# A transformer block in one kernel: one low half made by VectorE in two pairs, the z split moved into the fourth pick, and the last two tiles' roots by Sqrt and one Newton step

## The reference

```python
x  = hidden_states                              # 2048 tokens x 512, f32
d  = x @ gate_w.T - local_point                 # width 128
a  = x @ up_w.T @ local_approx.T + sum_m ((sign d)^m |d|^m / m! * (x @ up_w.T) [* (|d| <= 2.5) if m > 4]) @ fuse_m.T   # m = 1..6
f  = silu(x @ ffn_gate_w.T) * (x @ ffn_up_w.T) @ ffn_down_w.T          # width 1248
x1 = layernorm(x + a + f)
s  = x1 @ c1.T @ c2.T                           # rank 16, 1792 columns
idx = argmax of s in each block of 32 columns   # 56 winners per token
h  = relu(w1[idx] . x1)
out = layernorm(x1 + h @ w2t[idx])
```

## Time and profile before

| | us |
|---|---|
| time before, median of 3 runs (719.85 to 720.08) | 719.88 |
| the profiled execution's own time | 720.04 |
| its span, first to last instruction | 718.2 |
| TensorE busy | 705.4 (98%) |
| VectorE busy | 527.7 (73%) |
| ScalarE busy | 267.5 (37%) |
| GpSimd busy | 293.1 (41%) |

### The profile page before, as it was taken

How to read it: one execution, slowest core, us unless ns; L and a number is a source line. 1 busy time by engine, 2 the same in 40 slices (tenths; PEclk the granted TensorE clock), 3 DMA queues, 4 the chain that set the end, 5 groups by cost and what they waited for, 6 DMA issues and landing times.

```text
span 718.2 us, 10310 instructions
## 1 busy us (share of the span) xinstructions
PE 705.4 (98%) x3949; PEld 380.4 (53%) x3949; DVE 527.7 (73%) x983; ACT 267.5 (37%) x451; POOL 293.1 (41%) x278
## 2 busy tenths in 40 slices
PE   8999999999999999999999999999999999999996
PEld 3444444444444444444444456666666666667763
DVE  6979897796887779677778878948885778337236
ACT  1575457435721221222112224434334333443341
POOL 0452443211111161334215576897366435742330
PEclk9999999999999999999999999999999999999999
DMA  9637319300000110110010222121222101220101
GB/s 325 260 139 198 59 13 377 80 21 39 1 15 19 22 21 0 35 20 20 6 16 19 50 49 50 40 54 16 50 74 64 47 4 59 61 45 2 58 2 59
DMA packets 40833, 44.67 MB, mean 62 GB/s; under 512 B 25296, under 2 KB 33104, under 8 KB 39888
## 3 DMA queue, kind: packets, MB, share of 16 engines
q1 hardware_dynamic: 37808, 39.29, 18.0%
q0 software_dynamic: 2112, 4.19, 3.5%
q10 hardware_dynamic: 864, 0.53, 0.2%
HBM read 34.33 MB, written 4.42 MB: 54 GB/s over the span
## 4 chain that ended last, share of the span: by engine, by line
PE 73%; DVE 7%; POOL 5%; issue 2%; ACT 1%; DMA 0%; POOLq 0%; DVEq 0%; ACTq 0%
PE acc L544 27%; PE pb L524 14%; PE pa L524 13%; PE pb L778 7%; PE pa L778 6%; PE acc L621 2%; PE acc L867 1%; DVE big L1707 1%; POOL work L1127 1%; PE pick_a L687 1%; PE pick_b L687 1%; POOL quad L1181 1%; DVE small L1596 1%; POOL big L1134 1%; DVE big L1705 1%
## 5 line engine op out<-in xcount | busy, mean ns | idle before, releaser
L544 PE MATMUL acc<-big,work 128*128 128x512 f16 x1038 | 235.2, 379 | 1.5 <-POOL work L1127 1.5
L1127 POOL TENSOR_TENSOR work<-work 128x512 f16<-128x512 f32 x92 | 110.4, 1212 | 274.1 <-ACT work L1013 214.3
L544 PEld LDWEIGHTS acc<-big,work 128*128 128x128 f16 x1038 | 101.4, 98 | 117.3 <-POOL work L1127 2.0
L524 PE MATMUL pa<-xs,big 128*128 128x512 f16 x480 | 111.2, 379 | 0.0
L524 PE MATMUL pb<-xs,big 128*128 128x512 f16 x480 | 110.1, 379 | 0.0
L1838 DVE TENSOR_TENSOR pa<-pa,big 128x512 f32<-128x512 f32 x28 | 19.6, 699 | 83.4 <-ACT big L1093 69.0
L524 PEld LDWEIGHTS pa<-xs,big 128*128 128x128 f16 x480 | 46.1, 98 | 54.1
L524 PEld LDWEIGHTS pb<-xs,big 128*128 128x128 f16 x480 | 46.0, 98 | 53.4
L621 PE MATMUL acc<-big 128*128 128x512 f16 x336 | 73.8, 379 | 0.4 <-DVE big L1443 0.2
L1013 ACT ACTIVATE work<-work 128x512 f16<-128x512 f32 x40 | 25.2, 629 | 111.5 <-DVE work L1580 111.5
L1134 POOL TENSOR_TENSOR big<-work,big 128x512 f16<-128x512 f32 x27 | 36.8, 1378 | 64.1 <-ACT big L949 63.8
(11 more groups left out here) (214 smaller groups left out, 981.5 us busy)
## 6 DMA issues: line engine op xcount, KB each, us to landing
big<-in_w_all SPq DMA_DIRECT2D x2, 3840.0 KB, 17.4
big<-in_x_t SPq DMA_DIRECT2D x16, 256.0 KB, 8.2
rows<-in_x POOLq DMA_DIRECT2D x4, 1024.0 KB, 11.9
big<-spread_rows SPq DMA_DIRECT2D x16, 256.0 KB, 5.9
big<-in_w_all SPq DMA_DIRECT2D x2, 1536.0 KB, 11.5
big<-spread_rows SPq DMA_DIRECT2D x16, 192.0 KB, 5.1
out<-rows SPq DMA_DIRECT2D x3, 1024.0 KB, 4.4
big<-in_w_all SPq DMA_DIRECT2D x1, 2048.0 KB, 14.7
```

The lines of the kernel that those rows point to most:

```text
L524: mm = nc.tensor.matmul(dst[:, :], weights(wp)(kc * P, P), x_part16(g, xp, kc), start=(kc == 0 and wp == xp), stop=(kc == KC - 1 and wp == 1))
L544: mm = nc.tensor.matmul(acc[t][:, :], act_part(pair, j, ap, t * P, P), weights(wp)(0, H), start=(first and ap == wp), stop=(last and ap == 1))
L1127: nc.gpsimd.tensor_tensor(act_part(pair, j, 1), act32[j], act_part(pair, j, 0), ALU.subtract).then_inc(act_lo, 1)
```

## The change

1. **A low half by VectorE.** `LOW_BY_DVE = (4, 5)`. For sparse units 4 and 5 VectorE makes the low half of j = 0 (`low_first`) and raises a new semaphore `first_lo`, for which TensorE waits ahead of that product. In unit 4 it stands behind the low half of x1, in unit 5 between two picks. GpSimd makes j = 1 alone, after a wait for `first_lo`, and raises `act_lo` by two.
2. **The z split moves.** `pick` is cut in two, `find_hits` and `rank_hits`. In units 9, 12, 14, 17 and 18 the z split of the next tile stands between them in pick 3; that next unit has none at its head.
3. **The last two tiles.** The inverse square root of tile 2 and of tile 3 comes from ScalarE's Sqrt of variance + eps, VectorE's reciprocal and one Newton step (three instructions). ScalarE runs one Sqrt on a constant ahead of its last rows, and its order becomes: rows of tiles 0 and 1, root of tile 2, rows of tile 2, root of tile 3. VectorE takes and measures half 0 of the last tile inside the work on tile 2. Tiles 0 and 1 keep `size_rows`.

```diff
+LOW_BY_DVE = (4, 5)
...
-                    pe.wait_ge(act_lo, N1 + before * 2 + j + 1)
+                    if j == 0 and before in LOW_BY_DVE:
+                        pe.wait_ge(first_lo, LOW_BY_DVE.index(before) + 1)
+                    else:
+                        pe.wait_ge(act_lo, N1 + before * 2 + j + 1)
...
+            def root(t):
+
+                act.wait_ge(ve_ready, t - 1)
+                act.activation(ya[:, t:t + 1], ve[:, t:t + 1], ACT.Sqrt).then_inc(root_ready, 1)
+
+            act.activation(c1_inv, const_sb[:, 4:5], ACT.Sqrt, scale=0.0)
+            act.wait_ge(rows_sized, 1)
+            scale_row(0)
+            scale_row(1)
+            root(2)
+            act.wait_ge(rows_sized, 2)
+            scale_row(2)
+            root(3)
...
-                    else:
+                    elif n not in LOW_BY_DVE:
                         low(GROUPS * U1 + n, j, m)
+                    elif j:
+                        pool.wait_ge(first_lo, LOW_BY_DVE.index(n) + 1)
+                        low(GROUPS * U1 + n, j, m, 2)
...
-                cut_z(tile, pick_a)
+                if g * U1 + u - 1 not in JOB_IN_SWIGLU or u == 2:
+                    cut_z(tile, pick_a)
                 swiglu(g, u, 0)
...
                 if nxt is not None:
-                    pick(tile, 3, pick_b)
+                    find_hits(tile, 3, pick_b)
+                    if g * U1 + u in JOB_IN_SWIGLU and g * U1 + u < GROUPS * U1 - 1:
+                        cut_z(nxt, pick_a)
+                    rank_hits(tile, 3)
...
+            def low_first(n):
+
+                pair = GROUPS * U1 + n
+                dve.wait_ge(act_hi, N1 + 2 * n + 1)
+                v.tensor_tensor(act_part(pair, 0, 1), act32[0], act_part(pair, 0, 0), ALU.subtract).then_inc(first_lo, 1)
...
+                if n in LOW_BY_DVE and n not in PICKS_AT:
+                    low_first(n)
                 if n in PICKS_AT:
                     tile, k = PICKS_AT[n]
                     pick(tile, k, pick_a)
+                    if n in LOW_BY_DVE:
+                        low_first(n)
                     pick(tile, k + 1, pick_b)
...
+            size_rows(0, 2, rows_sized)
+            take(3, sparse_ready, hid_out, [2])
+            moments(3, 2, [2])
+            start_root(2)
+            take_half(0)
+            invert_root(2)
+            size_half(0)
+            refine_root(2)
+            v.scalar_tensor_tensor(out=row_shift[:, 2:3], in0=mv[:, 2, 0:1], scalar=-1.0, in1=y[:, 2:3],
+                                   op0=ALU.mult, op1=ALU.mult).then_inc(rows_sized, 1)
+            take_half(1)
+            size_half(1)
             settle()
-            step(v.bn_aggr(mv[:, TPG - 1, :], small[:, (TPG - 2) * 6:TPG * 6]))
-            size_rows(TPG - 1, TPG)
+            step(v.bn_aggr(mv[:, TPG - 1, :], small[:, 0:2 * 6]))
+            start_root(3)
+            invert_root(3)
+            refine_root(3)
```

More of the change, by code:

```diff
@@ L326, in program @@
         act_lo, peak_ready, term_lo = sem("act_lo"), sem("peak_ready"), sem("term_lo")
+        first_lo = sem("first_lo")
         fuse_lo = sem("fuse_lo")
@@ L339, in program @@
         rows_sized, last_row_out = sem("rows_sized"), sem("last_row_out")
+        ve_ready, root_ready = sem("ve_ready"), sem("root_ready")
         W1_BEFORE = 2
@@ L1114, in _, with scale_row, low @@
                     hidden(g, u)
-            for t in range(TPG - 1):
+            def scale_row(t):
                 tile = (GROUPS - 1) * TPG + t
-                act.wait_ge(rows_sized, max(t, 1))
                 act.activation(rows[:, tile, :], rows[:, tile, :], ACT.Identity, bias=row_shift[:, t:t + 1],
                                scale=y[:, t:t + 1]).then_inc(rows_out, 1)
+            def root(t):
[9 more added lines that the diff above has]
+            root(3)
         @block.gpsimd
         def _(pool):
-            def low(pair, j, n):
+            def low(pair, j, n, halves=1):
                 pool.wait_ge(act_hi, n + 1)
-                nc.gpsimd.tensor_tensor(act_part(pair, j, 1), act32[j], act_part(pair, j, 0), ALU.subtract).then_inc(act_lo, 1)
+                nc.gpsimd.tensor_tensor(act_part(pair, j, 1), act32[j], act_part(pair, j, 0), ALU.subtract).then_inc(act_lo, halves)
             def terms_low(g):
@@ L1693, in cut_z, with find_hits @@
                 v.tensor_tensor(pieces(6, 2), wide(z_rest, 2), pieces(3, 2), ALU.subtract).then_inc(z_cut, 1)
-            def pick(tile, k, src):
+            def find_hits(tile, k, src):
                 q = tile * PICKS + k
@@ L1700, in pick @@
                 h = hit[b].rearrange("p (b j) -> p b j", j=SPARSITY)
-                r = rank[b].rearrange("p (b j) -> p b j", j=SPARSITY)
                 dve.wait_ge(score_ready, q + 1)
@@ L1705, in pick, with rank_hits @@
                 v.tensor_tensor(h, s, block_max[b].unsqueeze(2).broadcast_to([P, PB, SPARSITY]), ALU.is_equal).then_inc(score_used, 1)
+            def rank_hits(tile, k):
+                q = tile * PICKS + k
+                b = k % 2
+                h = hit[b].rearrange("p (b j) -> p b j", j=SPARSITY)
+                r = rank[b].rearrange("p (b j) -> p b j", j=SPARSITY)
                 dve.wait_ge(score_used, PICKS + q + 1)
@@ L1713, in pick @@
                     step(last)
+            def pick(tile, k, src):
+                find_hits(tile, k, src)
+                rank_hits(tile, k)
             def w2_low(c0, c1):
@@ L1875, in _, with start_root, invert_root @@
                     normalise(g - 1, rows_out, mask=(g, u + 1))
-            for t in range(TPG - 1):
+            def start_root(t):
+                settle()
+                v.tensor_scalar(ve[:, t:t + 1], mv[:, t, 1:2], EPS, None, ALU.add).then_inc(ve_ready, 1)
+                step(v.tensor_scalar(spare[:, t:t + 1], mv[:, t, 1:2], EPS, -0.5, ALU.add, ALU.mult))
+            def invert_root(t):
+                dve.wait_ge(root_ready, t - 1)
+                step(v.reciprocal(y[:, t:t + 1], ya[:, t:t + 1]))
@@ new lines, in refine_root, with take_half @@
+            def refine_root(t):
+                y_, ya_ = y[:, t:t + 1], ya[:, t:t + 1]
+                settle()
+                step(v.tensor_tensor(ya_, y_, y_, ALU.mult))
+                settle()
+                step(v.tensor_tensor(ya_, ya_, spare[:, t:t + 1], ALU.mult))
+                settle()
+                step(v.scalar_tensor_tensor(out=y_, in0=ya_, scalar=1.5, in1=y_, op0=ALU.add, op1=ALU.mult))
+                settle()
+            def take_half(h):
+                r = rows[:, GROUPS * TPG - 1, h * HALF:(h + 1) * HALF]
+                dve.wait_ge(sparse_ready, GROUPS * TPG + h)
+                v.scalar_tensor_tensor(out=r, in0=last_halves[h], scalar=hid_out, in1=r,
+                                       op0=ALU.mult, op1=ALU.add).then_inc(banks_added, 1)
@@ L1877, in _, with size_half @@
+            def size_half(h):
+                dve.wait_ge(banks_added, added(2, GROUPS - 1, TPG - 1) + h)
+                step(v.bn_stats(stats[:, h, :], rows[:, GROUPS * TPG - 1, h * HALF:(h + 1) * HALF]))
+            for t in range(2):
                 take(3, sparse_ready, hid_out, [t])
                 moments(3, 2, [t])
[L1879 to L1887, removed]
+            size_rows(0, 2, rows_sized)
```

## The result

The changed kernel takes 715.56 us (median of 5 runs, 715.17 to 715.94) against 719.88 before (5 runs, 719.85 to 720.39). The ratio is 0.9933 with a 95% interval of 0.9921 to 0.9944, which puts the time at 715.1. The forecast was 716.2 with a range from 715.5: the direction and all three places were right, and the change won more than was forecast, so that by the ratio the time lies under the range (the median by itself, 715.56, lies just inside it). In the profiled execution (715.60 us, span 713.8) 4.44 us are gone from the span, where I had summed 3.85.

The account below looks back on a forecast made before the run. Bound: TensorE's own stream, with waits for one transposition and two low halves, plus the end behind its last product. 720.04 - 1.4 (z split) - 1.45 (low halves) - 1.0 (end) = 716.2 us; range 715.5 to 717.9.

Parts of the forecast that it names:

- TensorE, free since 398.79 (400.24 - 1.45): Before unit 18's scores: TensorE was taken as idle 1.45 us, waiting for the z transposition, until 400.24.
- Gain 0.76 + 0.69 = 1.45: Sparse units 4 and 5: TensorE's waits for GpSimd's low halves of pairs 4 and 5 both go, winning 1.45 us.
- the 0.05 that I had left standing at the z split: Unit 17: remainder of TensorE's 1.45 us wait for the transposition after the forecast gain of 1.4.
- all of it, 1.45: Upper bound for the gain in unit 17: TensorE's whole wait of 1.45 us goes.
- The z split: Unit 17: split starts 1.49 us earlier, at 394.41, GpSimd holds it about 0.1, done 1.39 earlier; gain 1.4.
- the wait goes all the same: Unit 17's transposition took 3.2 us, median 2.2; if what held it strikes elsewhere, TensorE's wait still goes.
- I cost these moves at nothing.: Splits moved in the other four units cost 0: rank and winner, 1.49 us, fit VectorE's 1.51 idle.
- the first rival: Unit 18: gating product uses up its 1.23 us reserve, giving back 0.1 to 1.0; 716.3 to 717.2; no separate chance.
- The low halves: Sparse units 4 and 5: VectorE's subtraction holds GpSimd up to 0.69 us per unit, within TensorE's reserve; gain 1.45.
- The end: Last tiles: half 1 starts 0.5 us earlier, ten root steps shrink from 1.79 to 1.28; gain 1.0, bounds 0.5 and 1.15.
- price without the cover of half 0 would be 0.5: Last tiles: without half 0 running beside tile 2's Sqrt, the new end would cost 0.5 us.
- the slower rival: Five moved splits make VectorE wait inside pick 3, TensorE then waits for gating products: 6.9 us lost, 723.1; chance 0.04.

Follow-up runs that it names:

- e6_roots: Kernel before with only the roots of tiles 2 and 3 by Sqrt and one Newton step, last tile's halves in the old order: 718.71 us, ratio 0.9976.

## Why the forecast came out low

- **What bounds the kernel.** Right: TensorE's stream, three waits in it, and the stretch behind it. 3.39 of the 4.44 came from the waits and 1.15 from the stretch; 0.10 was given back by the start-up.
- **"TensorE, free since 398.79 (400.24 - 1.45)" and "Gain 0.76 + 0.69 = 1.45".** This is the step that failed, in size only. I took the idle column for the length of a wait. Start to start the waits were 1.61, 0.93 and 0.86. With the 0.05 that I had left standing at the z split this is 0.54 of the sum's shortfall of 0.59 (the end adds 0.15, the start-up takes 0.10), and it also capped my bounds ("all of it, 1.45"), so that the range stopped too early. By the ratio 4.8 us were won (4.0 to 5.7); the rest of the distance to the 4.44 of the traces lies inside that interval and is not explained.
- **The z split.** The mechanism was right: start at 394.4, held once by GpSimd for 0.21 (I took 0.1), done 1.31 earlier by the trace and 1.41 against TensorE, whose products stand 0.10 later here. Against a wait of 1.61 that would have left 0.2; the landing took 2.7 us and not 3.2 and closed it. I had written that the wait goes all the same if the delay strikes elsewhere. It struck the same tile and cost less, which I had not foreseen, so here the forecast mechanism had help. (Tiles 10 and 11 in the last parts of the prediction should read 9 and 10: unit 18 routes tile 9.)
- **"I cost these moves at nothing."** Right for units 9, 12 and 14 and wrong for 18. Alone, the move in 17 loses 0.86 again one unit later. That is the first rival at work, by a cause that I had not named in it: not the gating product, but the next z split at its old place. The change was spared it because it moved that split too.
- **The low halves.** Both waits went and none came back. The lock was there, as the Trainium skill has it ("SBUF — State Buffer", "Who interferes with whom"): 1.21 for VectorE's subtraction against the 0.69 of the earlier trace rows, and 1.06 for a GpSimd pass. It lay in TensorE's reserve. Its price for GpSimd was 0.33 in unit 4 and 0.44 in unit 5, against my 0.69. (GpSimd's j = 1 was due at 481.4 by my own terms, not at 481.3; nothing hung on it.)
- **The end.** 1.15 against 1.0, within the bounds. Half 1 starts on time (0.58 won, 0.5 forecast), the root costs 1.20 and not 1.28 (0.59 won, 0.5 forecast); the reciprocal took 0.16 (I took 0.2) and the hand-overs 0.03 and 0.04. The text's "price without the cover of half 0 would be 0.5" is wrong: e6_roots has no such cover and loses nothing.
- **The rivals.** No rival came true in the whole change. The end did not hand its gain to ScalarE: the small step, Sqrt and both hand-overs take 0.42 (709.60 to 710.02). (The border of the slower rival should read 5.1, 721.3 - 716.2, and not 5.3.)

## What to carry to other kernels

Size a wait of a pipelined engine by the distance from start to start, set against the same pair of instructions at a place with no wait; the idle column takes its beginning from a modelled end, and here hid 0.16 or 0.17 us of each of the three waits. When one late step is moved forward, look at the next instance of the same step: the engine that was freed arrives there earlier too, and meets it at its old place. And before two edits to one chain are credited with a sum, try each: here the shorter roots alone gave all of it, and the reordering alone cost 0.33.

## What the runs showed of the hardware

A round trip from VectorE to ScalarE and back with a one-column Sqrt costs 0.42 us with the first VectorE instruction in it, little more than two small VectorE steps at 0.195. The table load of 1.28 us is followed by the first Sqrt after 0.02 us, as these two rows of ScalarE in the changed kernel show:

```profile
697.05 1.28 ACT L1132 ACT_TABLE_LOAD   x1
698.35 0.20 ACT L1132 ACTIVATE sc<-const_sb 128x1 f32<-128x1 f32 x1
```

A reciprocal of one column takes 0.16 us on VectorE, as much as a multiplication. A last store of half the bytes, issued separately, ends 0.14 us sooner behind its scaling (2.31 against 2.45), which the second scaling uses up.
